# Attention on one core: two scalings one unit later, and one swapped rotation split over a pair's border

## The chip, the cores and the metric

One core of a Trainium2 chip runs the whole program. The metric is the device time of one execution in microseconds (us), the median of several. The engines are PE (TensorE, matrix products), DVE (VectorE), ACT (ScalarE), POOL (GpSimd) and SP (SyncE, which issues the DMAs). They run in parallel, each in its own order, and wait for each other by semaphores that only count up.

## The reference

The input x is 2 x 512 tokens of width 512. Two blocks follow, each with a layer norm before and after it and a residual sum: an attention with low-rank factors, and a gated feed-forward. The change lies in the attention alone:

```python
q = _rmsnorm(h @ Wq_a, q_a_ln_w) @ Wq_b              # rank 192, 32 heads of 128 + 64
ckv = h @ Wkv_a                                      # 64 compressed + 64 rotated
kv = _rmsnorm(ckv[..., :64], kv_a_ln_w) @ Wkv_b      # k_nope 128 and v 128 per head
q_pe, k_pe = _apply_rope(q_pe, cos, sin), _apply_rope(k_pe, cos, sin)
scores = einsum('bhqd,bhkd->bhqk', qf, kf) * scale   # causal, softmax over the keys
o = einsum('bhqk,bhkd->bhqd', probs, v)
return o @ Wo
```

_apply_rope is xp * cos + rotate_half(xp) * sin: each rotated half of a query needs the other half times a sine.

## The kernel before, in words

Keys are never expanded: each head's query is taken into the compressed space of 64 numbers, so that its score is a product of 128 numbers (64 compressed, 64 rotated) with one key matrix that all heads share. Products are made in three parts, from a rounded high part and the rest as a low part of each factor (`three`, lines 1196 to 1198).

The 32 heads go in 16 **pairs** p. A pair has 16 **units** k: two batches, two heads, four blocks of 128 queries each, with 128 to 512 keys (i = k % 4). Units 0 to 7 are batch 1, that is queries gi = 4p+2 and 4p+3, one per head; units 8 to 15 of pair p serve batch 0 of the next pair in the rotations, queries 4p+4 and 4p+5. Every engine has a `body(p)` with the same loop over k, written out by hand, and each does for unit k what its order says, with the others two units ahead or behind:

- **PE** computes the scores of unit k+2 (L1196 to L1198, or L1252 for the first block), sometimes a product besides, and turns the probabilities of unit k (L1266). In unit 0 it turns the factors of the next pair into bank 5 (`turn_factors`, L1226; for the first pairs `absorb_query`, L1207), in unit 2 it does `multiply_factors` (L1218) into bank 6 and then the output product of batch 1 of the pair before (`output`, L1277), in unit 10 the output of batch 0. The queries of the next pair are made in units 5, 7, 13 and 15, into banks 6 and 7.
- **DVE** masks the scores of unit k+2 and takes their extreme (L817, with a short accumulator read behind it). Besides, it rotates queries: `rotate_swapped` multiplies the two swapped halves by the sine (L802, L803, 32 partitions each, out to `qswp`), `rotate_own` multiplies the query by the cosine (L809, out to `qrot`) and raises `q_rotated`. `scale_o` (L833) multiplies an output by the inverse sums of its probabilities, which come back through a DMA into `rsb`, and raises `o_scaled`. `weights_lo` (L792, L793) makes the low parts of the next pair's weights.
- **ACT** takes the exponential of unit k+2 (L513), moves the turned probabilities (L521) and rounds the queries' high parts (L503).
- **POOL** adds the two rotations (L392, raises `pe_added`) and makes the low parts (L399).

In this text "the mask of unit n" is the one that DVE issues in its unit n, that is the mask of the scores of unit n+2. In unit 7 DVE inverts the sums, PE turns them, and SP sends them out to DRAM and back into `rsb` (L293, L298).

The waits that the change touches are these: `multiply_factors(w)`, called with w = p+2 for p from 1 to 13, waits before it overwrites bank 6, and the first product into bank 5 waits for a scaling:

```python
pe.wait_ge(a.q_rotated, 4 * w - 5)     # multiply_factors(w), unit 2
pe.wait_ge(a.o_scaled, 2 * p - 1)      # unit 0, before absorb_query or turn_factors
dve.wait_ge(a.r_in, 32 * (p + b + 1))  # scale_o(p, b)
if BACK[k] == 2 and not first:         # mask_and_max: units with a short ring
    dve.wait_ge(a.exp_made, U - 1)
```

rotate_own(gi, h) raises q_rotated to gi + 1.

Of the kernel before, what the change touches and what calls it, by code (L numbers as in the profile page):

```python
# [22 lines left out]
ALU = mybir.AluOpType  # L23
# [63 lines left out]
def build(nc, x_d, wa_d, lnw_d, cst_d, kcs_d, sq_d, sv_d, w13_d, bs_d, a13_d, a2_d, w2_d, b2_d, out_d):  # L87
# [14 lines left out]
    sin1 = cst[:, 2 * SEQ:3 * SEQ]  # L102
# [20 lines left out]
    qswp = att.take("qswp", [P, 2, SEQ])  # L123
# [86 lines left out]
    bank = [nc.alloc_psum_tensor(f"bank{i}", [P, 512], F32) for i in range(8)]  # L210

    def weight(q, part):

        if q in (6, 7):
            return wv2[:, q - 6, part, :]
        return wv[:, (13, 12, 11, 10, 9, 8, None, None, 3, 2, 1, 0, 7, 6, 5, 4)[q], part, :]
# [13 lines left out]
    def o_bank(b):  # L230

        return bank[4] if b else bank[XB]
# [33 lines left out]
    with block:  # L266
# [206 lines left out]
        def _(act):  # L473
# [81 lines left out]
            def second_deviation(u):  # L555
                act.wait_ge(c.dve_step, 9 * u + 7)
                nc.scalar.activation(st2[:, 8:9], st2[:, 7:8], ACT.Sqrt, bias=eps_ln).then_inc(c.std2_made, 1)
# [181 lines left out]
            for hf in range(2):  # L739
                for n in range(12):  # L740
                    G, rows = 12 * hf + n, RROWS[n // FOLD]
                    act.wait_ge(g.gate_made, G + 1)
                    if G >= 2:
                        act.wait_ge(g.gu_made, G - 1)
                    nc.scalar.activation(sg[0:rows, G % 2, :], bank[GATE[G % 3]][0:rows, :], ACT.Silu)\  # L745
                      .then_inc(g.silu_made, 1)
                    if G == 1:
                        second_deviation(TB - 1)
# [37 lines left out]
        def _(dve):  # L786

            def weights_lo(w):

                dve.wait_ge(a.wq_hi_made, w + 1)  # L790
                pv = absorbed(w)[:, 0:4 * RKV].rearrange("p (k h n) -> p k h n", k=2, h=2)
                nc.vector.tensor_tensor(w1_lo[:, :, 0:RKV], pv[:, 0], w1_hi[:, :, 0:RKV].bitcast(F32), ALU.subtract)  # L792
                nc.vector.tensor_tensor(w2[64:P, :, 0:RKV], pv[64:P, 1], w2[64:P, :, 0:RKV].bitcast(F32), ALU.subtract)\  # L793
                  .then_inc(a.wq_split, 1)

            def rotate_swapped(gi, h, first=False):

                dve.wait_ge(a.q_made, gi + 1)
                if not first:
                    dve.wait_ge(a.pe_added, gi - 1)  # L800
                G = bank[6 + h]
                nc.vector.tensor_tensor(qswp[64:96, h, :], G[96:128, :], sin1[96:128, :], ALU.mult)  # L802
                nc.vector.tensor_tensor(qswp[96:128, h, :], G[64:96, :], sin1[64:96, :], ALU.mult)  # L803

            def rotate_own(gi, h, first=False):
                if not first:
                    dve.wait_ge(a.qt_split, gi - 1)
                    dve.wait_ge(a.s_made, QB * (gi - 2) + 1)
                nc.vector.tensor_tensor(qrot[:, h, :], bank[6 + h][:, :], cos1, ALU.mult).then_inc(a.q_rotated, 1)  # L809

            def mask_and_max(U, k, first=False):

                n = P * (k % QB + 1)
                dve.wait_ge(a.s_made, U + 1)
                if BACK[k] == 2 and not first:
                    dve.wait_ge(a.exp_made, U - 1)
                nc.vector.tensor_tensor_reduce(out=ss[:, RING[k], 0:n], in0=bank[k % 2][:, 0:n], in1=mask[:, SEQ - n:SEQ],  # L817
                                               scale=-SCALE, scalar=3.4e38, op0=ALU.add, op1=ALU.min,
                                               accum_out=negmax[:, k % 8:k % 8 + 1]).then_inc(a.s_masked, 1)

            def invert(p):

                n = UNITS if p == PAIRS else 2 * UNITS
                dve.wait_ge(a.exp_made, PU * p + n - UNITS if p < PAIRS else PU * PAIRS)
                if p:
                    dve.wait_ge(a.r_made, p)
                nc.vector.reciprocal(rinv[:, 0:n], sums(p)[:, 0:n]).then_inc(a.rinv_made, 1)

            def scale_o(p, b):

                dve.wait_ge(a.r_in, 32 * (p + b + 1))
                dve.wait_ge(a.o_made, 2 * p + b + 1)
                nc.vector.tensor_tensor(ot[:, b * QB:(b + 1) * QB, p, :],  # L833
                                        o_bank(b)[:, :].rearrange("p (t n) -> p t n", t=QB),
                                        rsb[:, 1 - b, :].rearrange("p (t n) -> p t n", t=QB), ALU.mult).then_inc(a.o_scaled, 1)

            def split_weights(q):

                raw = wv_raw[:, q // 2 % 3, q % 2, :]
                if q < 6:  # L840
                    dve.wait_ge((c.wv_in0, c.wv_in1, c.wv_in2)[q // 2], 16)
                    nc.vector.tensor_copy(weight(q, 0), raw).then_inc(c.wv_copied, 1)
                    dve.wait_ge(c.wv_copied, q + 1)
                else:
                    dve.wait_ge(c.wv_hi_made, q - 5)
                nc.vector.tensor_tensor(weight(q, 1), raw, weight(q, 0).bitcast(F32), ALU.subtract)\
                  .then_inc(c.wv_split, 1)

            def split_output(t, hh):

                dve.wait_ge(c.o_hi_made, 2 * t + hh + 1)
                nc.vector.tensor_tensor(o_s[:, hh, 1, :, :], ot[:, t, 8 * hh:8 * hh + 8, :],  # L852
                                        o_s[:, hh, 0, :, :].bitcast(F32), ALU.subtract).then_inc(c.o_split, 1)
# [8 lines left out]
            def body(p, first=False, last=False):  # L862
                for k in range(PU):
                    n = k + 2
                    if n < PU or not last:
                        mask_and_max(PU * p + n, n % PU)
                    if k == 7:
                        invert(p)
                    if last and k == 15:
                        invert(PAIRS)  # L870
                    if last and k == 7:
                        split_output(0, 0)
                    if last and k >= 8:
                        split_weights(k - 8)
                    b, r, gi = (1, k, 4 * p + 2) if k < UNITS else (0, k - UNITS, 4 * p + 4)
                    if k < UNITS or not last:
                        if first and k in (1, 2):
                            rotate_swapped(gi + k - 1, k - 1)
                            if k == 1:
                                rotate_own(gi, 0)  # L880
                        elif first and k == 3:
                            weights_lo(p + 1)
                            rotate_own(gi + 1, 1)
                        elif r == 1:
                            rotate_swapped(gi + 1, 1)
                        elif r in (0, 2) and not (first and k == 0):
                            rotate_own(gi + r // 2, r // 2)
                        if k == 2 and not first and not last:
                            weights_lo(p + 1)
                        if r == 7 and not last:  # L890
                            rotate_swapped(gi + 2, 0)
                    if k == 13 and not first:
                        scale_o(p - 1, 1)
                    if k == (13 if first else 14):
                        scale_o(p, 0)

            nc.vector.memset(sums(0)[:, 0:UNITS], 1.0)
            nc.vector.memset(eps_ln, LN_EPS)
# [20 lines left out]
            for t in range(TB + 4):  # L919
# [47 lines left out]
                if t in (TB, TB + 3):  # L967
                    h = (t - TB) // 3
                    rotate_swapped(h, h, first=True)
                    rotate_own(h, h, first=True)  # L970

            dve.wait_ge(early_out[4], 16)
            body(0, first=True)
            for p in range(1, PAIRS - 1):
                body(p)
            body(PAIRS - 1, last=True)
            split_weights(8)
            split_weights(9)
# [129 lines left out]
            for hf in range(2):  # L1108
                for n in range(12):
                    G, rows = 12 * hf + n, RROWS[n // FOLD]  # L1110
# [497 lines left out]
```

## Time and profile before

| | us |
|---|---|
| median of 3 runs | 568.68 |
| the three runs | 573.58, 568.68, 567.83 |
| profiled execution | 568.9 |
| its span, first to last instruction | 567.1 |
| PE busy | 553.4 (98%) |
| DVE busy | 444.7 (78%) |
| ACT busy | 395.2 (70%) |
| POOL busy | 212.3 (37%) |

Busy times are of one profiled execution; engines overlap, so they don't add up. PE's matmuls are pipelined and their ends are modelled, so its share says how full its queue is, not how close it is to its peak. The attention's pairs fill the span from about 43 us to about 406 us; the rest is the prologue before and the projection and feed-forward behind. The granted clock of PE was 0.999 of full speed over the span.

### The profile page before, as it was taken

To read this page: it belongs to the slowest core of one execution; us is meant where nothing else is said; L and a number is where in the kernel's file an instruction comes from. 1 tells how busy PE (TensorE), PEld (TensorE's weight loads), DVE (VectorE), ACT (ScalarE), POOL (GpSimd) and SP (SyncE) were. 2 spreads that over 40 slices of the span, in tenths; PEclk is the share of its full clock that TensorE was granted. 3 is DMA by queue.
4 is the path that set the end of the run, shared out by engine and by line. 5 is a ranking of instruction groups with operands and counts; after the bars stand their busy time and mean duration, and the time that the engine had idled before them with its cause. 6 is when DMAs were issued, how large, how long until landed. Compare 5 with 4: busy or idle time off the path is not lost. (4 is left out here: it accounts for less than half of the span.)

```text
span 567.1 us, 10780 instructions
## 1 busy us (share of the span) xinstructions
PE 553.4 (98%) x3265; PEld 422.2 (74%) x3265; DVE 444.7 (78%) x1184; ACT 395.2 (70%) x1171; POOL 212.3 (37%) x221
## 2 busy tenths in 40 slices
PE   8999999999999999999999999999999999999996
PEld 7677778777787787778878867876778888755565
DVE  5978777787688777877887777888878989885476
ACT  4767778787888787878878877888745554274353
POOL 3225454344444543444344435533011112135730
PEclk9999999999999999999999999999999999999999
DMA  9912322313313233112112111013691000001003
GB/s 331 407 57 69 100 72 94 98 35 100 124 40 99 68 97 99 35 57 70 34 39 72 32 39 30 20 46 127 204 352 56 1 15 1 0 1 57 1 30 120
DMA packets 21690, 47.20 MB, mean 83 GB/s; under 512 B 2425, under 2 KB 5249, under 8 KB 21377
## 3 DMA queue, kind: packets, MB, share of 16 engines
q1 hardware_dynamic: 21632, 46.50, 25.0%
q8 instruction: 28, 0.46, 0.3%
q14 instruction: 30, 0.24, 0.1%
HBM read 40.06 MB, written 6.43 MB: 82 GB/s over the span
## 5 line engine op out<-in xcount | busy, mean ns | idle before, releaser
L817 DVE CUSTOM_DVE_ANT_0 ss<-bank,cst 128x128 f32<-128x128 f32 (+3 forms) x256 | 125.2, 490 | 68.6 <-PE bank L1198 45.2
L521 ACT ACTIVATE pt<-bank 128x128 f32<-128x128 f32 (+3 forms) x256 | 110.4, 431 | 60.4 <-PE bank L1266 60.2
L513 ACT ACTIVATE pr<-ss,small 128x128 f32<-128x128 f32 (+3 forms) x256 | 143.4, 560 | 10.3 <-DVE small L817 8.9
L392 POOL TENSOR_TENSOR qrot<-qrot,qswp 64x512 f32<-64x512 f32 x64 | 82.0, 1282 | 115.1 <-DVE qrot L809 112.7
L1266 PE MATMUL bank<-ident,pr 128*128 128x128 f32 x640 | 113.6, 275 | 0.6 <-ACT pr L513 0.5
L1266 PEld LDWEIGHTS bank<-ident,pr 128*128 128x128 f32 x640 | 78.5, 141 | 21.9 <-issue 5.3
L399 POOL TENSOR_TENSOR qt_lo<-qrot,qt_hi 128x384 fp32r<-128x384 f32 x64 | 64.6, 1009 | 70.8 <-ACT qt_hi L503 69.6
L1196 PE MATMUL bank<-kt_hi,qt_hi 128*128 128x256 f32 (+2 forms) x192 | 80.9, 421 | 1.4 <-POOL qt_lo L399 0.7
L1277 PE MATMUL bank<-pt,kvn 128*64 128x256 f32 (+3 forms) x512 | 75.2, 434 | 0.7 <-ACT pt L521 0.7
L1277 PEld LDWEIGHTS bank<-pt,kvn 128*64 128x64 f32 x512 | 38.5, 137 | 39.4 <-issue 30.5
L1198 PE MATMUL bank<-kt_hi,qt_lo 128*128 128x256 f32 (+2 forms) x192 | 65.1, 339 | 0.0
L1197 PE MATMUL bank<-kt_lo,qt_hi 128*128 128x256 f32 (+2 forms) x192 | 64.8, 337 | 0.0
L1196 PE MATMUL bank<-wv,o_s 128*128 128x512 f32 x128 | 51.5, 402 | 0.0
L1198 PE MATMUL bank<-wv,o_s 128*128 128x512 f32 x128 | 50.5, 395 | 0.0
L1197 PE MATMUL bank<-wv,o_s 128*128 128x512 f32 x128 | 50.4, 394 | 0.0
L513 ACT ACTIVATION_READ_ACCUMULATOR pr<-ss,small 128x1 f32 x256 | 49.9, 195 | 0.0
L802 DVE TENSOR_TENSOR qswp<-bank,cst 32x512 f32<-32x512 f32 x64 | 44.5, 696 | 2.0
L803 DVE TENSOR_TENSOR qswp<-bank,cst 32x512 f32<-32x512 f32 x64 | 44.2, 691 | 0.9
L809 DVE TENSOR_TENSOR qrot<-bank,cst 128x512 f32<-128x512 f32 x64 | 43.9, 686 | 0.1
L448 POOL TENSOR_TENSOR half<-xn 128x256 f32<-128x256 f32 x7 | 8.1, 1156 | 89.9 <-ACT xn L565 79.9
L1196 PEld LDWEIGHTS bank<-kt_hi,qt_hi 128*128 128x128 f32 x192 | 36.4, 190 | 5.1 <-issue 1.6
L1198 PEld LDWEIGHTS bank<-kt_hi,qt_lo 128*128 128x128 f32 x192 | 36.1, 188 | 2.8
(191 smaller groups left out, 1103.6 us busy)
## 6 DMA issues: line engine op xcount, KB each, us to landing
rsb<-rinv_scratch SPq DMA_DIRECT2D x32, 256.0 KB, 4.0
sv<-sv SPq DMA_DIRECT2D x9, 576.0 KB, 5.5
sqa<-sq SPq DMA_DIRECT2D x16, 320.0 KB, 3.0
wv_raw<-wvo_scratch SPq DMA_DIRECT2D x8, 512.0 KB, 4.4
sve<-sv SPq DMA_DIRECT2D x7, 576.0 KB, 10.1
wvo_scratch<-vs SPq DMA_DIRECT2D x10, 256.0 KB, 3.1
xa<-x SPq DMA_DIRECT2D x8, 256.0 KB, 6.5
sqr<-sq SPq DMA_DIRECT2D x16, 128.0 KB, 2.1
```

The source lines that it names most:

```text
L392: nc.gpsimd.tensor_tensor(qrot[RKV:P, h, :], qrot[RKV:P, h, :], qswp[RKV:P, h, :], ALU.add)\
L399: nc.gpsimd.tensor_tensor(qt_lo[:, b, h, P:SEQ], qrot[:, h, P:SEQ], qt_hi[:, b, h, P:SEQ].bitcast(F32), ALU.subtract)\
L513: nc.scalar.activation(pr[:, k % 4, 0:n], ss[:, RING[k], 0:n], ACT.Exp, bias=negmax[:, k % 8:k % 8 + 1], scale=-1.0, accum_out=sum_of(U // ...
L521: nc.scalar.activation(pt[:, b, h, 0:i + 1, i * P:(i + 1) * P], bank[2 + k % 2][:, 0:(i + 1) * P].rearrange("p (j q) -> p j q", q=P), ACT. ...
L802: nc.vector.tensor_tensor(qswp[64:96, h, :], G[96:128, :], sin1[96:128, :], ALU.mult)
L803: nc.vector.tensor_tensor(qswp[96:128, h, :], G[64:96, :], sin1[64:96, :], ALU.mult)
L817: nc.vector.tensor_tensor_reduce(out=ss[:, RING[k], 0:n], in0=bank[k % 2][:, 0:n], in1=mask[:, SEQ - n:SEQ], scale=-SCALE, scalar=3.4e38, ...
L1196: nc.tensor.matmul(out, w_hi, x_hi, start=start, stop=False)
L1197: nc.tensor.matmul(out, w_hi, x_lo, start=False, stop=False)
L1198: return nc.tensor.matmul(out, w_lo, x_hi, start=False, stop=stop)
L1266: last = nc.tensor.transpose(bank[2 + k % 2][:, j * P:(j + 1) * P], pr[:, k % 4, j * P:(j + 1) * P], ident[:, :])
L1277: last = nc.tensor.matmul(o_bank(b)[RKV * h:RKV * (h + 1), j * P:SEQ], kvn[:, QB * b + j, 0:RKV], pt[:, b, h][:, j, j * P:SEQ], start=(j = ...
```

## The change

On DVE, in every pair but the first and last, the scaling of batch 1 of the pair before moves from unit 13 to unit 14, and that of this pair's batch 0 from unit 14 to unit 15; in unit 15 it now stands behind the mask and before the rotation. In the first pair the one scaling moves from unit 13 to 15; in the last pair both stand in unit 14. `rotate_swapped` gets a list of parts. Of the swapped rotation of the next pair's first query (gi = 4p+6, unit 15) only the first half (into partitions 64 to 96) stays in unit 15; the second half is done in unit 0 of the next pair, behind its mask and before rotate_own. The two rotations in unit 7 stay together. No operation is added or dropped.

```diff
-            def rotate_swapped(gi, h, first=False):
+            def rotate_swapped(gi, h, first=False, parts=(0, 1)):
...
-                G = bank[6 + h]
-                nc.vector.tensor_tensor(qswp[64:96, h, :], G[96:128, :], sin1[96:128, :], ALU.mult)
-                nc.vector.tensor_tensor(qswp[96:128, h, :], G[64:96, :], sin1[64:96, :], ALU.mult)
+                for j in parts:
+                    to, of = 64 + 32 * j, 96 - 32 * j
+                    nc.vector.tensor_tensor(qswp[to:to + 32, h, :], bank[6 + h][of:of + 32, :], sin1[of:of + 32, :], ALU.mult)
...
+                    if k == 14 and not first:
+                        scale_o(p - 1, 1)
+                    if k == (14 if last else 15):
+                        scale_o(p, 0)
                     b, r, gi = (1, k, 4 * p + 2) if k < UNITS else (0, k - UNITS, 4 * p + 4)
...
+                        elif k == 0 and not first:
+                            rotate_swapped(gi, 0, parts=(1,))
+                            rotate_own(gi, 0)
                         elif r in (0, 2) and not (first and k == 0):
                             rotate_own(gi + r // 2, r // 2)
...
                         if r == 7 and not last:
-                            rotate_swapped(gi + 2, 0)
-                    if k == 13 and not first:
-                        scale_o(p - 1, 1)
-                    if k == (13 if first else 14):
-                        scale_o(p, 0)
+                            rotate_swapped(gi + 2, 0, parts=(0, 1) if k == 7 else (0,))
```

## Rows read from the trace of the kernel before

**Rows 1.** Waits, 60 to 390 us: engine, line, waited-for line: us in total, times, longest.
```profile
DVE ss L817 <- PE bank L1198: 44.7, 96, 1.2
...
DVE ot L833 <- DMA rsb<-rinv_scratch: 2.2, 1, 2.2
...
PE bank L1252 <- DVE small L817: 0.9, 1, 0.9
...
ACT qt_hi L503 <- POOL qrot L392: 0.3, 1, 0.3
```

**Rows 2.** Timeline of DVE, border of pairs 6 and 7: start, us, instruction, idle before.
```profile
201.00 0.69 DVE L833 TENSOR_TENSOR ot<-bank,rsb 128x512 f32<-128x512 f32 x1
201.65 0.29 DVE L817 CUSTOM_DVE_ANT_0 ss<-bank,cst 128x128 f32<-128x128 f32 x1
...
201.86 0.69 DVE L833 TENSOR_TENSOR ot<-bank,rsb 128x512 f32<-128x512 f32 x1
202.65 0.42 DVE L817 CUSTOM_DVE_ANT_0 ss<-bank,cst 128x256 f32<-128x256 f32 x1
203.00 0.08 DVE L817 DVE_READ_ACCUMULATOR2_ANT small<- 128x1 f32 x1
203.11 0.70 DVE L802 TENSOR_TENSOR qswp<-bank,cst 32x512 f32<-32x512 f32 x1
203.82 0.69 DVE L803 TENSOR_TENSOR qswp<-bank,cst 32x512 f32<-32x512 f32 x1
204.53 0.56 DVE L817 CUSTOM_DVE_ANT_0 ss<-bank,cst 128x384 f32<-128x384 f32 x1
...
205.01 0.69 DVE L809 TENSOR_TENSOR qrot<-bank,cst 128x512 f32<-128x512 f32 x1
```

**Rows 3.** Timeline of PE over the same border.
```profile
201.22 0.39 PE L1252 MATMUL bank<-kt,qrot 128*128 128x128 f32 x2
...
204.06 0.34 PE L1198 MATMUL bank<-kt_hi,qt_lo 128*128 128x384 f32 x1
204.23 0.27 PE L1226 MATMUL bank<-ident,wt 128*128 128x128 f32 x1
```

**Rows 4.** Timeline of ACT there: the end of an exponential.
```profile
202.32 0.19 ACT L513 ACTIVATION_READ_ACCUMULATOR pr<-ss,small 128x1 f32 x1
```

**Rows 5.** Timeline of PE's weight loads (PEld) there, start of unit 2.
```profile
205.37 0.30 PEld L1252 LDWEIGHTS bank<-kt,qrot 128*128 128x128 f32 x2
205.81 0.23 PEld L1218 LDWEIGHTS bank<-sqa 128*64 128x64 f32 x4
```

**Rows 6.** The same at the border of pairs 0 and 1.
```profile
69.35 0.30 PEld L1252 LDWEIGHTS bank<-kt,qrot 128*128 128x128 f32 x2
69.77 0.20 PEld L1218 LDWEIGHTS bank<-sqa 128*64 128x64 f32 x4
```

**Rows 7.** DVE there: the own rotation.
```profile
68.34 0.69 DVE L809 TENSOR_TENSOR qrot<-bank,cst 128x512 f32<-128x512 f32 x1
```

**Rows 8.** DVE in the first pair: swapped half with own rotation behind.
```profile
43.21 0.69 DVE L803 TENSOR_TENSOR qswp<-bank,cst 32x512 f32<-32x512 f32 x1
43.91 0.69 DVE L809 TENSOR_TENSOR qrot<-bank,cst 128x512 f32<-128x512 f32 x1
```

**Rows 9.** Timeline of DVE, border of pairs 12 and 13.
```profile
335.56 0.69 DVE L833 TENSOR_TENSOR ot<-bank,rsb 128x512 f32<-128x512 f32 x1 [2.18 <-DMA rsb<-rinv_scratch]
...
339.32 0.69 DVE L809 TENSOR_TENSOR qrot<-bank,cst 128x512 f32<-128x512 f32 x1
```

**Rows 10.** Timeline of PE's weight loads there.
```profile
339.52 0.30 PEld L1252 LDWEIGHTS bank<-kt,qrot 128*128 128x128 f32 x2 [1.13 <-issue]
340.13 0.23 PEld L1218 LDWEIGHTS bank<-sqa 128*64 128x64 f32 x4 [0.30 <-issue]
```

**Rows 11.** Timeline of DVE in pair 14: the mask of unit 3.
```profile
365.32 0.42 DVE L817 CUSTOM_DVE_ANT_0 ss<-bank,cst 128x256 f32<-128x256 f32 x1
```

**Rows 12.** Timeline of PE in pair 14, unit 5.
```profile
365.98 0.48 PE L1196 MATMUL bank<-kt_hi,qt_hi 128*128 128x512 f32 x1
```

## The prediction

> **What bounds the kernel now.** The page comes first, but TensorE's busy share rests on modelled ends, so I went on to the waits of the attention stage (60 to 390 us). There VectorE waits for TensorE's scores 96 times and TensorE shows one of note, 0.9 us [rows 1]: TensorE sets the pace and the others follow. The third view was the timeline of every engine over one boundary between two pairs (unit 15 of pair 6, units 0 and 1 of pair 7), because all edits lie there. The question for each edit is then: does it make a TensorE instruction start later, and if so, is that given back?
>
> VectorE around the boundary [rows 2] runs, in order of start: scaling 201.00, mask of unit 14 at 201.65, scaling 201.86, mask of unit 15 at 202.65, the two halves of the swapped rotation at 203.11 and 203.82, mask of unit 0 at 204.53, own rotation 205.01 to 205.70. The two scalings sit in holes. The mask of unit 14 couldn't start before its scores, issued at 201.22 and 0.39 long [rows 3], so at 201.61; the mask of unit 15 waits for the exponential whose last part runs 202.32 to 202.51 [rows 4], and starts 0.14 behind it. From 202.65 to the end of the own rotation VectorE has no hole of more than a tenth.
>
> The own rotation is what matters there. In unit 2 TensorE does multiply_factors (L1218), which overwrites bank 6 and waits for q_rotated >= 4w-5 with w = p+2, that is 4p+3: exactly the own rotation of query 4p+2 in unit 0. Its first weight load starts at 205.81, 0.11 behind the rotation's end; it comes 0.44 behind the load for the scores in front of it [rows 5]. At the boundary of pairs 0 and 1 the same distance is 0.42 (69.35 to 69.77) although the rotation had ended at 69.03 [rows 6, 7]. So TensorE's queue and the rotation meet within 0.02 to 0.03 us: there is no slack to absorb a later rotation.
>
> **The change part by part.**
>
> *Scaling of batch 1, from unit 13 to unit 14.* It leaves 201.00 and takes the place of the other at 201.86. What it frees stays empty, since the mask of unit 14 waits for its scores until 201.61. Gain 0, cost 0. Nobody waits soon for its o_scaled: the output that needs it comes a pair later.
>
> *Scaling of batch 0, from unit 14 to unit 15.* It now stands behind the mask of unit 15. That one is held by ScalarE and doesn't come earlier. A scaling starts with the accumulator read (as at 201.00), so at 203.00, and the next operation 0.65 to 0.71 later (a scaling with a mask behind it; a swapped half with another behind it) [rows 2]: 203.65 to 203.71. Its signal o_scaled releases turn_factors, which runs at 204.23 [rows 3]; the scaling ends at 203.69. Cover 0.5 us, cost 0.
>
> *Half of the swapped rotation, from unit 15 to unit 0.* The first half runs from 203.71 to 204.40, so the mask of unit 0 may start at 204.43, when its scores end (204.06 + 0.34 [rows 3]): 0.10 earlier than now. The accumulator read follows 0.48 later, the second half 0.11 after that (as 203.00 to 203.11): 205.02. The own rotation comes 0.70 behind a swapped half [rows 8]: 205.72 instead of 205.01, **0.71 later**. Put otherwise: VectorE gets 0.69 of work into a stretch without holes, and what it gave up was a hole.
>
> [...]
>
> *What the later rotation holds back.* L1218 waits for it, and TensorE's queue is in order: the output product of the pair before and all scores behind it wait too. Its load moves from 205.81 to 205.72 + 0.69 + 0.11 = 206.52, 0.71 less the slack of up to 0.03: I take **0.70 us per pair**, all on the path. It isn't given back. Behind it VectorE (0.71 late), ScalarE and GpSimd stand to TensorE as before, and from unit 3 on each waits again for TensorE, as now. GpSimd's addition follows the rotation, and ScalarE's rounding of the query follows that; both move with the rest.
>
> *How often.* multiply_factors is called for p = 1 to 13. For p = 2 to 12, eleven times, 0.70 each: 7.7. At p = 1 TensorE has the long absorb_query in front, and the rotation ended 0.74 before L1218's first load: 0.71 later it ends at 69.74, and with 0.11 behind it the load comes at 69.85 instead of 69.77, so 0.1. At p = 13 the profiled execution had a late transfer: the scaling in unit 13 waited 2.18 us for rsb until 335.56, and L1218's first load ran at 340.13, behind a rotation that ended at 340.01 [rows 9, 10]. In the new order VectorE stands at that transfer too, one mask further: scaling 335.56, mask 336.17, scaling 336.52, half 337.23, mask 337.94, half 338.53, rotation 339.23. That is 0.09 earlier than now; 0. At p = 14 there is no L1218 to absorb the delay. It runs on through the second query and the weight operations, and the mask behind them moves from 365.32 to about 366.03; TensorE's scores of the unit, now at 365.98, need it, and the mask had ended 0.24 before them, of which 0.1 is the signal's way: 0.6 [rows 11, 12]. At p = 15 the next pair's weight operations are missing, which gives VectorE some room; I give it 0.1.
>
> *Edges.* In the first pair one scaling moves from unit 13 to 15 and is in the reckoning for p = 1. In the last pair both stand in unit 14, 0.6 to 1.2 later for one of them, with no rotation behind: 0. DMAs: none is moved; SyncE's order is untouched.
>
> **Sum.** 7.7 + 0.1 + 0 + 0.6 + 0.1 = 8.5 us. The profiled execution took 568.9, a span of 567.1 and 1.8 around it; it lies 0.2 above the median of the three runs (568.68). 568.7 + 8.4 (without the last tenths, which waits for other engines in the last pair may swallow) gives **577.1 us**. The bounds of the term per pair are 0.62 (the scaling at 0.65, the slack taken off) and 0.75 (two holds of 0.03 more): 7.0 to 8.3 for eleven. A late transfer that doesn't happen in the new kernel takes up to 2.2 off and puts 0.7 on; one more adds up to 1.5.
>
> **The rivals.**
>
> *Hidden after all.* L1218's distance to the load in front of it is nearly the same at p = 1, where it can't have waited. If its 0.11 is chance and the rotation has room, the delay first shows at the scores of unit 5 as at p = 14, but in a middle pair TensorE has the four loads of L1218 in front (0.23 [rows 5]), so 0.35 a pair is left: 11 x 0.35 + 0.8 = 4.7 us, 573.3. Against it: the wait is in the program, and at p = 13, where the rotation was late, the load came 0.12 behind its end and 0.61 behind the load in front [rows 9, 10]: 0.11 is how a real wait looks. It gets 8%.
>
> *Not slower, even faster.* The mechanism would be this: the split lets the mask of unit 0 start 0.10 sooner, and the later scalings give the transfer into rsb a unit more. It decides if TensorE waits for that mask or that transfer in many pairs. Both together are worth 13 x 0.1 + 2.2 = 3.5 us, 565.2, if the rotation costs nothing. [...] But the transfer was waited for once in 32 scalings, for 2.2 us [rows 1], and even then TensorE had to wait for the rotation behind. 2%.
>
> *Worse than reckoned.* The 0.71 also delays, through GpSimd's addition, ScalarE's queue, and a second wait of some 0.3 us per pair comes up behind L1218: 581. ScalarE waited for that addition only once, 0.3 us [rows 1], so there is room. 4%.
>
> **How the numbers follow.** The forecast, 0.62 to 0.75 per pair, has 86%; hidden 8%, faster side 2%, worse 4%. About 1% of the time, 5.7 us, is what a measurement of this kernel can tell from no change. The range, 574.5 to 579.5, holds the bounds of the term with one late transfer more or fewer. Slower by over 1% (above 574.4) gets 0.90: the forecast and the worse case; within 1% 0.08; faster 0.02.
>
> **What the changed profile would show.** In a middle pair: the scaling in unit 13 gone and VectorE idle there for about 0.5 us; two scalings before and behind the mask of unit 15; swapped halves on both sides of the mask of unit 0, the second 0.11 behind its accumulator read, the rotation 0.70 behind that; L1218 about 0.70 later behind the load in front of it, at 1.14 instead of 0.44, and the pair's period up by 0.7. At p = 14 a hole before the scores of unit 5. I am wrong if L1218 keeps its 0.44, or if the period grows by less than 0.5.

## The result, and the profile after

| | before | after |
|---|---|---|
| median, us | 569.68 (4 runs) | 577.62 (4 runs: 576.99 to 577.80) |
| profiled execution, us | 568.9 | 576.99 |
| its span, us | 567.1 | 575.2 |

The ratio is 1.015, with an interval of 1.0126 to 1.0174: the change makes the kernel 1.5% slower. This ratio is on record as that of the fast runs; the two medians alone, with the spread of before (567.83 to 573.58), would give 1.014. The median of before is now that of the three runs shown ahead and a fourth of 570.68. The forecast was 577.1 us, on a base of 568.7. The experiments ran on three chips (1 to 4 on one, 5 and 7 to 9 on the second, 6 and the second profile of 1 on the third), on which the kernel before has medians of 568.5 to 568.8. One execution of the first experiment's kernel, the profiled one, took 2399 us; why was not found, and it is left out. The kernel's profile was then taken from another execution.

"The scores of unit n" are below, as in the prediction, those that TensorE makes in its unit n. In the changed kernel's trace the lines of TensorE's code lie three further down: multiply_factors is L1221, the scores of a first block L1255, other scores L1199 to L1201. Both swapped halves are now line 803.

VectorE over the border of pairs 6 and 7, the timeline that answers to [rows 2]; the columns are start in us, length in us, instruction, and the idle time before it with what ended it:

```profile
205.37 0.29 DVE L817 CUSTOM_DVE_ANT_0 ss<-bank,cst 128x128 f32<-128x128 f32 x1 [0.57 <-PE bank L1255]
205.59 0.08 DVE L817 DVE_READ_ACCUMULATOR2_ANT small<- 128x1 f32 x1
205.59 0.69 DVE L833 TENSOR_TENSOR ot<-bank,rsb 128x512 f32<-128x512 f32 x1
206.37 0.42 DVE L817 CUSTOM_DVE_ANT_0 ss<-bank,cst 128x256 f32<-128x256 f32 x1
206.72 0.08 DVE L817 DVE_READ_ACCUMULATOR2_ANT small<- 128x1 f32 x1
206.72 0.69 DVE L833 TENSOR_TENSOR ot<-bank,rsb 128x512 f32<-128x512 f32 x1
207.44 0.69 DVE L803 TENSOR_TENSOR qswp<-bank,cst 32x512 f32<-32x512 f32 x1
208.16 0.56 DVE L817 CUSTOM_DVE_ANT_0 ss<-bank,cst 128x384 f32<-128x384 f32 x1
208.64 0.08 DVE L817 DVE_READ_ACCUMULATOR2_ANT small<- 128x1 f32 x1
208.76 0.69 DVE L803 TENSOR_TENSOR qswp<-bank,cst 32x512 f32<-32x512 f32 x1
209.46 0.69 DVE L809 TENSOR_TENSOR qrot<-bank,cst 128x512 f32<-128x512 f32 x1
```

From the mask of unit 15 to the own rotation it is 3.09 us (206.37 to 209.46); before it was 2.36 (202.65 to 205.01). Where the first scaling stood, VectorE now waits 0.57 us for the scores of L1255. So 0.73 us of work moved out of a hole and in front of the rotation.

TensorE's weight loads at the same border, answering to [rows 5]:

```profile
209.09 0.30 PEld L1255 LDWEIGHTS bank<-kt,qrot 128*128 128x128 f32 x2
210.27 0.23 PEld L1221 LDWEIGHTS bank<-sqa 128*64 128x64 f32 x4 [0.87 <-issue]
```

The distance was 0.44, it is 1.18. The load comes 0.12 behind the rotation's end (209.46 + 0.69 = 210.15), as it came 0.11 behind it before. The waits of 60 to 390 us, answering to [rows 1], show the same wait once per pair:

```profile
PEld bank L1221 <- issue: 10.9, 13, 1.1
PE bank L1221 <- DVE qrot L809: 8.8, 12, 1.0
...
DVE ot L833 <- DMA rsb<-rinv_scratch: 0.5, 1, 0.5
```

One pair long windows, the kernel after and then the kernel before: span, busy time of TensorE, its loads, VectorE, ScalarE, GpSimd, then clock, DMA share and GB/s:

```profile
204.98:228.38 23.40, 22.69 (x150) 17.63 (x149) 17.71 (x49) 18.24 (x61) 10.08 (x10) 1.00 0.28 79
```

```profile
201.00:223.68 22.68, 22.68 (x148) 17.61 (x147) 17.58 (x50) 18.28 (x61) 10.08 (x10) 1.00 0.28 84
```

TensorE is busy for the same 22.7 us; the pair is 0.72 us longer, and TensorE is not busy in 0.71 of it. The clock is the same.

Where the 8.1 us of the span came from can be read off the first weight load of multiply_factors, border by border, and behind the last of them off the scores of unit 5 (L1196, now L1199):

| place | before | after | later by | of which new |
|---|---|---|---|---|
| L1218, pair 1 | 69.77 | 69.82 | 0.05 | 0.05 |
| L1218, pair 12 | 316.62 | 324.73 | 8.11 | 8.06, in 11 borders |
| L1218, pair 13 | 340.13 | 347.69 | 7.56 | -0.55 |
| scores of unit 5, pair 14 | 365.98 | 374.11 | 8.13 | 0.57 |
| scores of unit 5, pair 15 | 387.28 | 395.51 | 8.23 | 0.10 |

At pair 14 the changed trace has the hole in front of the scores of unit 5, and behind pair 12 the late transfer is waited for again, at the scaling that now stands in unit 14 (answering to [rows 12] and [rows 9]):

```profile
374.11 0.50 PE L1199 MATMUL bank<-kt_hi,qt_hi 128*128 128x512 f32 x1 [0.24 <-DVE small L817]
343.21 0.69 DVE L833 TENSOR_TENSOR ot<-bank,rsb 128x512 f32<-128x512 f32 x1 [0.53 <-DMA rsb<-rinv_scratch]
```

### The profile page after: what moved, and what is told of

Read it like the earlier page. It is cut to its first block and busy times, and to the rows that moved or that the text cites. A ratio compares the mean times of both kernels' runs of the same rounds, so it can differ in the third digit from the quotient of the medians.

```text
span 575.2 us, 10795 instructions
## 1 busy us (share of the span) xinstructions
PE 554.1 (96%) x3265; PEld 423.1 (74%) x3265; DVE 446.0 (78%) x1184; ACT 394.5 (69%) x1171; POOL 212.3 (37%) x221
## 5 line engine op out<-in xcount | busy, mean ns | idle before, releaser
L1199 PE MATMUL bank<-kt_hi,qt_hi 128*128 128x256 f32 (+2 forms) x192 | 80.9, 421 | 1.6 <-DVE small L817 0.9
L1201 PE MATMUL bank<-kt_hi,qt_lo 128*128 128x256 f32 (+2 forms) x192 | 65.1, 339 | 0.0
L1199 PE MATMUL bank<-wv,o_s 128*128 128x512 f32 x128 | 51.5, 402 | 0.0
L1201 PE MATMUL bank<-wv,o_s 128*128 128x512 f32 x128 | 50.5, 395 | 0.0
L1199 PEld LDWEIGHTS bank<-kt_hi,qt_hi 128*128 128x128 f32 x192 | 36.4, 190 | 5.4 <-issue 1.6
L1201 PEld LDWEIGHTS bank<-kt_hi,qt_lo 128*128 128x128 f32 x192 | 36.0, 188 | 2.9
L1200 PEld LDWEIGHTS bank<-kt_lo,qt_hi 128*128 128x128 f32 x192 | 36.8, 192 | 0.0
```

The costliest lines, as they stand in the source:

```text
L1199: nc.tensor.matmul(out, w_hi, x_hi, start=start, stop=False)
L1200: nc.tensor.matmul(out, w_hi, x_lo, start=False, stop=False)
L1201: return nc.tensor.matmul(out, w_lo, x_hi, start=False, stop=stop)
```

## The experiments

All times are medians; the ratio is that to the kernel before, run beside it. "A pair takes" is the distance from one first weight load of multiply_factors to the next, in one trace.

**1. The scalings alone.** The split is undone, the scalings stay in units 14 and 15:

```diff
-                        elif k == 0 and not first:
-                            rotate_swapped(gi, 0, parts=(1,))
-                            rotate_own(gi, 0)
...
-                            rotate_swapped(gi + 2, 0, parts=(0, 1) if k == 7 else (0,))
+                            rotate_swapped(gi + 2, 0)
```

> The scalings stand in units 14 and 15 as in the changed kernel; the swapped rotation is whole again, in unit 15. My theory (work put into a stretch of VectorE without holes, in front of the own rotation that TensorE waits for): the rotation is as late as the added scaling is long less what overlaps, 0.6 us per pair, and now the mask of unit 0 is late too, so that TensorE waits first at the scores of unit 2 (0.4) and then at multiply_factors (0.2): 11 x 0.6 and about 0.5 in pair 14, less 0.9 for a milder late transfer at pair 12, 575.1 to 576. [...] Rival B, the two edits' costs add up, half each: 573.

576.14 us, ratio 1.013 (1.0113 to 1.0147). That is 0.1 above what I expected. Neither a loss by the split alone nor one by halves (rival B) shows: this edit alone brings nearly the whole loss. The profile of this kernel:

> The kernel of the first experiment again, for an undisturbed profile. My theory: in a middle pair the mask of unit 0 starts at about 0.6 us later behind the mask of unit 15 than in the changed kernel, TensorE's load for the scores of unit 2 waits for it by about 0.4, the own rotation starts 0.1 earlier than in the changed kernel, and the pair takes 23.28 us against 23.40; 575.8 to 576.3. If the pair takes 23.0 or less, the half in unit 0 carries a cost of its own.

575.71 us in that one execution, 0.1 below what I expected. Its weight loads at the border of pairs 6 and 7, and VectorE's mask of unit 0 and own rotation:

```profile
208.53 0.30 PEld L1252 LDWEIGHTS bank<-kt,qrot 128*128 128x128 f32 x2 [0.42 <-issue]
209.13 0.23 PEld L1218 LDWEIGHTS bank<-sqa 128*64 128x64 f32 x4 [0.31 <-issue]
```

```profile
207.85 0.56 DVE L817 CUSTOM_DVE_ANT_0 ss<-bank,cst 128x384 f32<-128x384 f32 x1
208.33 0.08 DVE L817 DVE_READ_ACCUMULATOR2_ANT small<- 128x1 f32 x1
208.33 0.69 DVE L809 TENSOR_TENSOR qrot<-bank,cst 128x512 f32<-128x512 f32 x1
```

TensorE waits in two places, 0.42 for the mask of unit 0 at the scores of unit 2, and again at multiply_factors. A pair takes 23.28 us, as expected. (The row of the load says only "issue"; the load starts 0.12 behind the end of that mask's accumulator read.)

**2. The split alone.** Scalings back in units 13 and 14:

```diff
-                    if k == 14 and not first:
-                        scale_o(p - 1, 1)
-                    if k == (14 if last else 15):
-                        scale_o(p, 0)
...
                             rotate_swapped(gi + 2, 0, parts=(0, 1) if k == 7 else (0,))
+                    if k == 13 and not first:
+                        scale_o(p - 1, 1)
+                    if k == (13 if first else 14):
+                        scale_o(p, 0)
```

> The swapped rotation is split as in the changed kernel; the scalings stand in units 13 and 14 as before. My theory: the place in unit 15 that the half leaves stays empty, since the mask of unit 0 can't start before its scores end; the half then stands alone in front of the own rotation. The rotation is as late as in the changed kernel, 0.73 us per pair: 11 x 0.73, 0.6 in pair 14, and the late transfer at pair 12 costs what it did before: 577 to 578, the same as the changed kernel. The costs of the two edits do not add up, since each alone takes away the same hole. Rival A (the scalings alone cost): 569. Rival B (half each): 573.

577.21 us, ratio 1.0156 (1.0141 to 1.0171): the loss of the whole change. VectorE behind the first half, at the border of pairs 6 and 7:

```profile
206.63 0.70 DVE L803 TENSOR_TENSOR qswp<-bank,cst 32x512 f32<-32x512 f32 x1
207.95 0.56 DVE L817 CUSTOM_DVE_ANT_0 ss<-bank,cst 128x384 f32<-128x384 f32 x1 [0.62 <-PE bank L1201]
208.44 0.08 DVE L817 DVE_READ_ACCUMULATOR2_ANT small<- 128x1 f32 x1
208.55 0.69 DVE L803 TENSOR_TENSOR qswp<-bank,cst 32x512 f32<-32x512 f32 x1
209.26 0.69 DVE L809 TENSOR_TENSOR qrot<-bank,cst 128x512 f32<-128x512 f32 x1
```

The place that the second half left stays empty for 0.62 us, since the scores aren't there; then it runs where TensorE waits for it. Alone 1.3% and 1.6%, together 1.5%: the two edits spend the same 0.6 to 0.7 us per pair, and it is paid once. In the full change the later scaling fills the hole that the split makes.

**3. The wait covered.** The changed kernel, with multiply_factors behind the output product:

```diff
                     if k == 2 and not first:
+                        output(p - 1, 1)
                         if p + 2 < PAIRS:
                             multiply_factors(p + 2)
-                        output(p - 1, 1)
```

> The changed kernel, but multiply_factors stands behind the output product in unit 2 instead of in front of it, so that 2.3 us of TensorE work cover the later rotation. My theory: L1221 no longer waits; the next thing that is late is the mask of unit 3, behind the weight operations, by 0.2 to 0.3 us per pair; with the milder late transfer 570 to 572. Rival: the cost is not in that wait but in VectorE's later masks or in the scalings' signal; then it stays at 576 to 578.

571.02 us, ratio 1.0047 (1.0030 to 1.0063). Two thirds of the loss is gone with the order of two TensorE products and nothing else. What is left, in the pair that begins at 205:

```profile
211.98 0.29 DVE L793 TENSOR_TENSOR w<-bank,w 64x128 fp32r<-64x128 f32 x1
212.31 0.43 DVE L817 CUSTOM_DVE_ANT_0 ss<-bank,cst 128x256 f32<-128x256 f32 x1
```

```profile
212.79 0.19 PEld L1199 LDWEIGHTS bank<-kt_hi,qt_hi 128*128 128x128 f32 x1 [0.30 <-DVE small L817]
```

The mask of unit 3 follows the weight operations without a gap and TensorE waits 0.30 for it; a pair takes 22.90 us.

**4. The same cover on the kernel before**, by the same exchange of lines.

> The kernel before, with multiply_factors behind the output product. My theory: the wait for the rotation costs the kernel before 0.01 to 0.03 us per pair, so nothing is gained: 568.4 to 569.5, same. Rival: TensorE already lost up to 0.1 us per pair at that wait (the distance of 0.31 us between the scores and L1218 against 0.22 elsewhere); then 567.5.

568.25 us, ratio 1.0003 (0.9984 to 1.0022): the same, 0.15 below what I expected. A pair goes from 22.68 to 22.63 us. I had taken 0.01 to 0.03. Whether the 0.05 is the wait's cost isn't shown: the exchange also changes the distances between the loads of the two products, and the distance of 0.44 against 0.42 where nothing was waited for speaks for 0.02. What the run does show is that the exchange by itself gains next to nothing, so that what experiment 3 gained is the wait.

**5. The rest covered too.** As 3, and the weight operations one unit later:

```diff
-                        if k == 2 and not first and not last:
+                        if k == 3 and not first and not last:
                             weights_lo(p + 1)
```

> The changed kernel with multiply_factors behind the output product, and the next pair's weight operations on VectorE moved from unit 2 to unit 3, into the hole behind that mask. My theory: the 0.25 us per pair left in the run with the late product alone is the mask of unit 3, pushed by the weight operations; with them out of the way nothing of the change is on the path, a middle pair takes 22.63 us as in the kernel before with the late product, and the late transfer at pair 12 costs about 0.4 instead of 0.9: 567.5 to 568.3. Rival: the rest is the later scaling's signal to turn_factors; then 570.5 to 571.

566.99 us, ratio 0.9974 (0.9965 to 0.9983): faster than both kernels, by 0.3% and 1.7% (0.9974 against 1.015). Pairs 2 to 8 take 22.63 us, as in 4. The signal of the later scaling costs nothing. The time is 0.5 below what I expected: the late transfer cost 0.03 us in this trace, not 0.4.

**6. The same two covers without the change.**

> The kernel before with the same two covers as the fastest kernel so far (multiply_factors behind the output product, weight operations in unit 3), scalings and rotation as before. My theory: on an undisturbed pair both take the same 22.63 us; what the later scalings are still worth is the late transfer at pair 12, 0.5 to 0.9 us: 567.6 to 568.3, against 567.0 with the change. If it takes 567.0 or less, the change is worth nothing even where it is covered.

568.06 us, ratio 0.9988 (0.9975 to 1.0001). Undisturbed pairs take 22.63 us here too. The difference of 1.1 us to experiment 5 lies at the border of pairs 12 and 13: from one first load of multiply_factors to the next it is 23.11 us here and 21.80 there, against 21.77 at the border before. Not all of these 1.3 us is the order's: from the store of the sums to the scaling that waits for them it took 8.24 us here and 7.84 there, so 0.4 is a transfer that happened to be later. In experiment 4, with the scalings in their old places and 7.75 us, the border took 22.63, still 0.86 above the 21.77 of the one before, where experiment 5 lost 0.03. So the later scalings do have a worth in these traces, some 0.9 us of tolerance for the late transfer, and in the change it was buried under the rotation. In whole executions it is less sure: 5 and 6 ran on different chips, and the intervals of their ratios overlap a little.

**7. The own rotation in front of the half.** A change of the group of partitions is here a start on other partitions than those of the operation before: a half is on 32 of them, a mask or an own rotation on all 128. The two helpers also return their instruction, which is not shown:

```diff
                         elif k == 0 and not first:
-                            rotate_swapped(gi, 0, parts=(1,))
-                            rotate_own(gi, 0)
+                            rotate_own(gi, 0, signal=False)
+                            rotate_swapped(gi, 0, parts=(1,)).then_inc(a.q_rotated, 1)
```

> The changed kernel, but in unit 0 the own rotation stands in front of the second swapped half, which raises the signal. Same work, one start less that changes the group of partitions right behind the accumulator read. My theory: the own rotation starts with the accumulator read, 0.48 behind the mask, the half follows when it has ended, and the signal comes about 0.1 us per pair earlier than in the changed kernel: 576.3. If such changes of group cost nothing, the sum of starts is the same: 577.6.

575.38 us, ratio 1.0120 (1.0107 to 1.0134). The border of pairs 6 and 7:

```profile
207.58 0.56 DVE L820 CUSTOM_DVE_ANT_0 ss<-bank,cst 128x384 f32<-128x384 f32 x1
208.07 0.08 DVE L820 DVE_READ_ACCUMULATOR2_ANT small<- 128x1 f32 x1
208.07 0.69 DVE L810 TENSOR_TENSOR qrot<-bank,cst 128x512 f32<-128x512 f32 x1
208.77 0.69 DVE L803 TENSOR_TENSOR qswp<-bank,cst 32x512 f32<-32x512 f32 x1
```

The rotation starts with the accumulator read, where the half had started 0.12 behind it. A pair takes 23.28 us instead of 23.40. The whole is 0.9 below what I expected; in the traces another 0.34 lies at the border of pairs 12 and 13 (22.62 against 22.96), and the rest stays open.

**8 and 9. The same extra work in two places.** One operation of 0.69 us more per pair, its output unused, once in unit 13 and once in unit 15:

```diff
+                    if k == 13 and not last:
+                        nc.vector.tensor_tensor(qswp[32:64, 1, :], cos1[32:64, :], sin1[32:64, :], ALU.mult)
                     if k == 14 and not first:
                         scale_o(p - 1, 1)
```

```diff
                     if k == (14 if last else 15):
                         scale_o(p, 0)
+                    if k == 15 and not last:
+                        nc.vector.tensor_tensor(qswp[32:64, 1, :], cos1[32:64, :], sin1[32:64, :], ALU.mult)
```

> The changed kernel with one more VectorE operation per pair (32 x 512, 0.69 us, its output unused), in unit 13, where the first scaling stood. My theory: it falls into the hole that the scaling left, 0.57 to 0.9 us, and costs at most 0.1 to 0.2 us in pairs 1 to 8 and nothing later: 577.6 to 578.8. Rival, VectorE's total work sets the pace: 0.69 x 15, about 588.

> The same extra operation, in unit 15 behind the scaling. My theory: it stands in the stretch without holes, so that every pair from 1 to 13 pays it in full, 0.6 to 0.72 us, and pair 14 at the scores of unit 5 as well: 577.6 + 13 x 0.68 = 586 to 587. Rival, the border has room for it: 577.6.

577.68 us in unit 13, ratio 1.0161 (1.0145 to 1.0176); 587.52 in unit 15, ratio 1.0335 (1.0321 to 1.0348). A pair takes 23.40 us with the extra operation in unit 13, as without it, and 24.09 with it in unit 15: 0.69 more, its own length. The second time is 0.5 above what I expected; the border of pairs 12 and 13, with the late transfer, grew by 1.11 instead of 0.69. In the first case the ratio is that of the changed kernel within its interval. In unit 13 it stands in the hole:

```profile
204.97 0.69 DVE L817 CUSTOM_DVE_ANT_0 ss<-bank,cst 128x512 f32<-128x512 f32 x1 [0.57 <-ACT pr L513]
205.58 0.08 DVE L817 DVE_READ_ACCUMULATOR2_ANT small<- 128x1 f32 x1
205.70 0.68 DVE L876 TENSOR_TENSOR qswp<-cst 32x512 f32<-32x512 f32 x1
206.39 0.29 DVE L817 CUSTOM_DVE_ANT_0 ss<-bank,cst 128x128 f32<-128x128 f32 x1
```

## Why the prediction was right

**The mechanism** held step by step. The scaling's old place stayed empty (0.57 idle in front of the mask of unit 14), the mask of unit 15 did not move up, the own rotation came later and L1218 with it at 0.12 behind its end, and nothing was given back: experiment 3, which takes away that wait, takes away most of the loss, while the same exchange gains next to nothing in the kernel before (experiment 4), and experiments 8 and 9 show that the place of the work decides and not its sum.

**The term per pair** was 0.70 and measured 0.73 (8.06 in 11 borders). I had taken a little off for slack, and there was none: in the kernel before the load already came 0.11 to 0.12 behind the rotation's end at all twelve borders from pair 2 on, as it does in the changed kernel. The rotation itself I had 0.71 later, and it is 0.73: the first half started 0.72 behind the scaling instead of 0.71, and the second 0.12 behind the accumulator read instead of 0.11. Over eleven borders that is 8.06 us instead of 7.7.

**The edges.** Pair 1: 0.1 predicted, 0.05 measured, or 0.12 if counted from the first load of absorb_query at 67.4 us, which came 0.07 earlier in the changed trace. Pair 14: 0.6 and 0.57, at the place named. Pair 15: 0.1 and 0.10. **Pair 13 is the term that was mis-sized**: I gave it 0, and it was -0.55. I had let the late transfer arrive at the same time in both kernels. The store of the inverse sums kept SyncE waiting 3.50 us there before and 3.05 after, so the transfer came 0.45 earlier, and 0.09 were in the reckoning. Experiment 8 has the changed order at this place too and a transfer 0.23 us later (8.20 us from store to scaling against 7.97), and its border is 0.23 longer, 23.19 against 22.96: the border follows the transfer. How late it is differs from trace to trace, so this term could have been priced only as a range. The terms sum to 8.2 as measured and to 8.5 as predicted; the spans differ by 8.1, the medians by 7.9. That the sum came so close is in part luck: 0.36 too little in the eleven borders stands against 0.55 too much at pair 13.

**The later starts.** That VectorE starts a half later than an own rotation was read from rows: 0.11 behind the mask's accumulator read, where the own rotation starts with it [rows 2]. In the changed trace there are four later starts per border (half behind scaling, mask behind half, half behind mask, rotation behind half), each 0.70 to 0.72 behind an operation of 0.69 or 0.12 behind an accumulator read. Experiment 7, with one such start less in front of the signal, is worth 0.12 us per pair; that start is then behind the signal, at the mask of unit 1 (0.72 behind the half). The upper bound of the term per pair, 0.75, has two holds of 0.03 in it that no run shows: the starts that the reckoning has 0.71 and 0.11 behind the operation before came 0.72 and 0.12 behind it, 0.01 more each. Without later starts at the half and at the rotation, that is with the half 0.48 behind its mask and the rotation 0.65 behind the half, the distances that [rows 2] show at 205.01 and 201.65, I estimate that the rotation would have come 0.55 later; it was 0.73.

**The rivals.** "Hidden after all" fell with the 1.18 between the loads. Its reckoning of what comes next, 0.35 us per pair at the scores of unit 5, was the right place: with the wait covered it is 0.27 (22.90 against 22.63 us). "Not slower" was right in one half: the later scalings do help at a late transfer, by some 0.9 us in experiment 5 against 6 and 4, once the rotation isn't in the way. "Worse" did not come: ScalarE waited for GpSimd's addition twice, 0.5 us in all.

What I had not said ahead is that the two edits' costs don't add. Either alone moves the rotation by 0.6 to 0.7 us. The later scaling puts 0.69 us of work into the stretch without holes. The split puts a half behind the mask of unit 0, and that mask moves up by only 0.1 us into the place that the half left, since its scores end then. Together, the scaling fills that place.

## What to carry to other kernels

Before moving an operation within an engine's order, ask what hole it leaves and what stands behind its new place: work that leaves a hole frees nothing, and in front of an operation that the bounding engine waits for it is paid in full (here 0.69 us of extra work cost nothing per pair in the hole and 0.69 us in front of the rotation, experiments 8 and 9). Look at that consumer first: here the order of two TensorE products was worth 1% of the kernel (a ratio of 1.0047 instead of 1.015), and only with that cover did the change show a gain, of some 0.9 us in the traces. Test two edits of one change each alone, and don't expect the costs to add: both may spend the same slack.

## What the runs showed of the hardware

The store of the inverse sums (8 KB) to DRAM at pair 12 is slow in eleven of eleven traces, those of all kernels here: SyncE issues the load behind it 3.04 to 3.57 us after the store, against 1.36 us in most pairs and 1.72 to 2.09 in pairs 2, 5 and 8. At pair 1 it is slow in four of them (3.05 to 3.45). The place repeats and the cause was not found; no run here tells a collision with another DMA from anything else.

An own rotation, which the profile shows as 0.69 us long, is followed by the next operation 0.60 us after its start where that one is on all 128 partitions too (own rotation at 205.01, mask of unit 1 at 205.61 in the kernel before): all 46 starts without idle time behind an own rotation in the pairs of that kernel are at 0.60 or 0.61. Where the partitions change it took 0.70 to 0.72 in the rows of the changed kernel's border shown above (206.72 to 207.44, 207.44 to 208.16, 208.76 to 209.46), and a half behind an own rotation came 0.70 after its start at all 15 borders of experiment 7. Two swapped halves behind one another, which have the same shape and are on different partitions, are 0.70 to 0.72 apart in the kernel before, so in these traces a change of shape is not needed for the later start.
